# Square sums of q and k in the first mixer: the selector held in four column tiles, the squares streamed

## The reference, cut to what matters

```python
q = _causal_conv_silu(x @ w_q, conv_q)      # k likewise
q = q * rsqrt(sum(q * q, -1) + 1e-6)        # k likewise
# per token t: S = S * exp(g_t); mem = k_t S; delta = (v_t - mem) * b_t
#              S = S + k_t delta;  o_t = q_t * scale @ S
```

## Time and profile before

| what | value |
|---|---|
| median of 3 runs | 5464.05 us (5441.55 to 5478.0) |
| profiled execution, span from first to last instruction | 5452.6 us |
| time of the profiled execution beside its span | not listed apart; the median of the runs is 11.45 us above the span |
| TensorE busy with matmuls | 4831.1 us, 89% of the span |
| VectorE, ScalarE, GpSimd busy | 70%, 50%, 42% |
| mean granted TensorE clock | 0.926 |

### The profile page before, as it was taken

The page is one execution under the profiler, slowest core; times in us unless marked ns, Lnnn a source line. Parts: engine busy times, 40 slices in busy tenths (PEclk is TensorE's granted clock), DMA queues, the critical chain, the costliest instruction groups (busy, mean ns, idle before and its releaser), DMA issues. The chain is left out here.

```text
span 5452.6 us, 104905 instructions
## 1 busy us (share of the span) xinstructions
PE 4831.1 (89%) x36890; PEld 3535.1 (65%) x36890; DVE 3836.5 (70%) x9111; ACT 2736.9 (50%) x6711; POOL 2285.8 (42%) x1860
## 2 busy tenths in 40 slices
PE   5999999999999999999889989984488778998998
PEld 3787777877777787777766556641156665654665
DVE  4766667777677766767578668746699657866874
ACT  2444445444544544545478658724400116875882
POOL 2434334344334434434267347514322116743751
PEclk7999999999999999999999999986699758998998
DMA  2000000000000000000100000000000000000000
GB/s 86 5 9 7 7 9 7 7 9 7 7 9 10 5 9 8 6 9 9 34 1 0 25 5 0 0 7 0 8 1 1 1 1 30 0 24 5 0 0 16
DMA packets 170085, 52.60 MB, mean 10 GB/s; under 512 B 142304, under 2 KB 166112, under 8 KB 168928
## 3 DMA queue, kind: packets, MB, share of 16 engines
q1 hardware_dynamic: 168160, 44.30, 3.7%
q10 hardware_dynamic: 1536, 3.21, 0.2%
HBM read 36.99 MB, written 10.49 MB: 9 GB/s over the span
## 5 line engine op out<-in xcount | busy, mean ns | idle before, releaser
L799 DVE SCALAR_TENSOR_TENSOR gd_qkT<-gd_ps,gd_w_qk,gd_qkT 128x256 f32<-128x256 f32 x768 | 367.2, 482 | 193.3 <-ACT gd_qkT L632 172.7
L984 POOL TENSOR_TENSOR gd_gV<-gd_g,cst 128x512 f32<-128x512 f32 x128 | 130.3, 1040 | 860.1 <-PE gd_ps L510 860.1
L417 PE MATMUL gd_ps<-gd_taps,gd_xwins 128*128 128x512 f32 x1024 | 465.3, 597 | 0.0
L676 ACT ACTIVATE gd_X<-gd_ps 128x512 f32<-128x512 f32 x384 | 201.1, 620 | 452.9 <-PE gd_ps L496 452.6
L1540 ACT ACTIVATE L_ffn_s<-L_ffn_s,L_ffn_nb,L_ffn_r 128x128 f32<-128x128 f32 x1024 | 419.4, 482 | 3.1
L1360 POOL TENSOR_TENSOR L_ffn_t<-L_ffn_t 128x512 f32<-128x512 f32 x128 | 190.2, 1486 | 391.8 <-DVE L_ffn_t L1581 391.8
L417 PEld LDWEIGHTS gd_ps<-gd_taps,gd_xwins 128*128 128x128 f32 x1024 | 192.8, 191 | 191.1 <-issue 185.6
L868 DVE TENSOR_TENSOR gd_Z<-gd_ps,cst 128x256 f32<-128x256 f32 x384 | 162.7, 424 | 129.6 <-PE gd_ps L512 111.1
L1579 DVE TENSOR_TENSOR L_ffn_t<-L_ffn_ps,L_ffn_sb_rope 128x512 f32<-128x512 f32 x256 | 176.8, 691 | 101.8 <-PE L_ffn_ps L1385 101.8
L521 PE MATMUL gd_ps<-gd_Z,gd_X 128*128 128x64 f32 x2048 | 239.2, 275 | 0.0
L512 PE MATMUL gd_ps<-gd_gV,gd_nA 128*128 128x64 f32 x2048 | 237.9, 275 | 0.0
(11 more groups left out here) (389 smaller groups left out, 13625.6 us busy)
## 6 DMA issues: line engine op xcount, KB each, us to landing
L_ffn_sb_rope<-in_rope SPq DMA_DIRECT2D x4, 2048.0 KB, 8.3
gd_tap_row<-in_L_attn_conv_v SPq DMA_DIRECT2D x2, 2048.0 KB, 15.6
gd_blocks<-gd_nA SPq DMA_DIRECT2D x256, 16.0 KB, 1.7
gd_Z<-gd_blocks SPq DMA_DIRECT2D x32, 128.0 KB, 2.0
gd_inverses<-gd_Z SPq DMA_DIRECT2D x32, 128.0 KB, 1.7
gd_gV<-gd_inverses SPq DMA_DIRECT2D x256, 16.0 KB, 1.9
L_ffn_sb_wqkv<-in_L_ffn_wqkv SPq DMA_DIRECT2D x4, 768.0 KB, 8.9
out<-out_tok SPq DMA_DIRECT2D x8, 256.0 KB, 2.6
```

The source lines that it names most:

```text
L417: ins = pe.matmul(ps[4 + i % 2][:], xwin(j)[:, t:t + P], taps[:, t, 512 * i:512 * (i + 1)], start=(t == 0), stop=(t == TAPS - 1))
L676: act.activation(heads(X, gi).rearrange("p h x -> p (h x)"), ps[4 + gi][:], ACT.Copy).then_inc(x_s.sem, 1)
L799: ins = dve.scalar_tensor_tensor(produced(j, i), ps[6 + i % 2][:, P + t:P + t + WIDE], w_tap[:, at, t:t + 1], produced(j, i), ALU.mult, AL ...
```

## The change

The selector becomes the stationary operand: 32 columns of it, of which four carry something, in one of four column tiles (output partitions 32z to 32z + 31); the squares of a whole pair (256 tokens) stream. Pair `i` goes to tile `z = i % 4`, and the two pairs of a tile are added into the same 32 rows of bank 6, with selectors in which different columns are filled. The result is head by token, in a 128x256 area. ScalarE copies it to `sums_by_head` in SBUF, TensorE turns it back by two 128x128 transposes into columns 256 to 511 of bank 6, and VectorE reads 32 columns from there. The eight matmuls now come in one go behind `turn_k`, with the waits for the four squares; the turning comes behind the second gate projection. On ScalarE the copy stands ahead of the four `silu_gate`. The signal `square_sums_mm` counts two per chunk.

```diff
-                def square_sums(turn, q):
-                    w(sq_s.now(turn, q))
-                    for i in (2 * q, 2 * q + 1):
-                        for c in range(2):
-                            at = SUMS.start + 2 * PAIRS * c + 2 * i
-                            ins = pe.matmul(ps[6][:, at:at + 2], qk_sq[:, i, P * c:P * (c + 1)], cst[:, C_HALVES:C_HALVES + 2], start=True, stop=True)
-                    if q == 3:
-                        ins.then_inc(ss_mm.sem, 1)
+                def square_sums(turn):
+                    for i in range(PAIRS):
+                        if i % 2 == 0:
+                            w(sq_s.now(turn, i // 2))
+                        x, z = divmod(i, 4)
+                        ins = pe.matmul(ps[6][32 * z:32 * (z + 1), 0:WIDE], cst[:, C_HALVES + 32 * x:C_HALVES + 32 * (x + 1)], qk_sq[:, i], start=(x == 0), stop=(x == 1))
+                    ins.then_inc(ss_mm.sem, 1)
+
+                def turn_square_sums(turn):
+                    w(sbh_s.now(turn))
+                    for c in range(2):
+                        ins = pe.transpose(ps[6][:, SUMS.start + P * c:SUMS.start + P * (c + 1)], sums_by_head[:, P * c:P * (c + 1)], ident)
+                    ins.then_inc(ss_mm.sem, 1)
...
                 def body(n, b, c, j, s, follows, more):
                     turn_k(n, j)
-                    for i in range(4):
-                        if follows:
-                            square_sums(n + 1, i)
-                        project_gate(n, j, i)
+                    if follows:
+                        square_sums(n + 1)
+                    project_gate(n, j, 0)
+                    project_gate(n, j, 1)
+                    if follows:
+                        turn_square_sums(n + 1)
+                    project_gate(n, j, 2)
+                    project_gate(n, j, 3)
...
+                def copy_square_sums(turn):
+                    w(ss_mm.now(turn, 0))
+                    act.activation(sums_by_head[:], ps[6][:, 0:WIDE], ACT.Copy).then_inc(sbh_s.sem, 1)
...
                     token_major_k(n)
+                    if follows:
+                        copy_square_sums(n + 1)
                     for i in range(4):
                         silu_gate(n, i)
```

More of the change, by code:

```diff
@@ L29 @@
 C_HALVES = C_EYE + BASE * BASE
-C_END = C_HALVES + 2
+C_END = C_HALVES + 2 * 32
 def constant_table():
@@ L42, in constant_table @@
         t[:, C_MERGE + 64 * n:C_MERGE + 64 * (n + 1)] = i[:, None] // s == cols[None, :] // s + 1
-    t[:, C_HALVES:C_HALVES + 2] = i[:, None] // HALF == np.arange(2)[None, :]
+    for x in range(2):
+        for y in range(2):
+            t[:, C_HALVES + 32 * x + 2 * x + y] = i // HALF == y
     t[:, C_EYE:C_EYE + BASE * BASE] = np.eye(BASE).reshape(1, -1)
@@ L255, in gated_delta @@
         delta = sb("delta", [P, H, DV])
+        sums_by_head = sb("sums_by_head", [P, WIDE])
         k_ss, k_inv, k_norm, q_eps = (sb(n, [P, 2, H]) for n in ("k_ss", "k_inv", "k_norm", "q_eps"))
@@ L289, in gated_delta @@
         qk_mm, tap0_s, conv_s, silu_s = sig("qk_mm", PAIRS), sig("first_tap", PAIRS), sig("convolved", PAIRS), sig("qk_silu", PAIRS)
-        sq_s, ss_mm, ss_s, inv_k_s, nrm_s = sig("squares", 4), sig("square_sums_mm", 1), sig("square_sums", 1), sig("k_inverse", 1), sig("k_norms", 1)
+        sq_s, ss_mm, ss_s, inv_k_s, nrm_s = sig("squares", 4), sig("square_sums_mm", 2), sig("square_sums", 1), sig("k_inverse", 1), sig("k_norms", 1)
+        sbh_s = sig("sums_by_head", 1)
         v_mm, v_out, vn_s = sig("v_mm", 4), sig("v_out", 4), sig("v_scaled", 4)
@@ L313, in gated_delta @@
         PROD = slice(P, P + XWIN)
-        SUMS = slice(448, 480)
+        SUMS = slice(WIDE, 2 * WIDE)
         SCORES = slice(32, 64)
@@ L608, in _ @@
                 w(conv_s.now(0))
-                for i in range(4):
-                    square_sums(0, i)
+                square_sums(0)
+                turn_square_sums(0)
                 w(ss_s.now(0))
@@ L738, in _ @@
                 silu(0, -2, PAIRS - 1)
+                copy_square_sums(0)
                 exp_ab(1)
@@ L808, in square_sums @@
                     w(ss_mm.now(turn))
-                    sums = ps[6][:, SUMS].rearrange("p (c k two) -> p c two k", two=2, k=4)
-                    by_head = lambda t: t[:].rearrange("p c h -> p (c h)").rearrange("p (c two k) -> p c two k", two=2, k=4)
+                    sums = ps[6][:, SUMS].rearrange("p (c z g) -> p c g z", c=2, z=4)[:, :, 0:4]
+                    by_head = lambda t: t[:].rearrange("p c (g z) -> p c g z", z=4)
                     if j % 2 == 0:
```

## The result

The changed kernel takes 5389.86 us (median of 4 runs, 5378.43 to 5394.78), the kernel before 5459.01 us in the same session (4 runs, 5441.55 to 5478.0). The ratio is 0.9867, 95% interval 0.9833 to 0.9902: faster by 1.3%, 69 us. I had forecast 27 us. The span of the profiled execution fell from 5452.6 to 5385.6 us, and 66.9 of these 67.0 us are gone at the last output product of the first mixer (2702.3 us before, 2635.4 us after).

What follows compares the result with a forecast made beforehand. TensorE, busy 89% of the span, bounds the kernel, with waits deciding which savings count. Path gain -32, clock loss +20 and clock gain -15 sum to -27 us: 5464 to 5437 us (5425 to 5450; low end 5405, high end 5475).

Steps and rivals of the forecast that it cites:

- B: Every second first-mixer chunk: TensorE waits 3.05 us for the last silu, then reaches `solve` without waiting; savings up to 3.1 us count.
- 15 chunks: 32 us: In B chunks, 2.1 us less TensorE work each counts in full, 32 us saved over 15 chunks.
- The price of the four tiles: Added square matmuls, first mixer: 16 records in four column tiles take 1.1 us, with 3.5 us as the other end.
- added waits: New waits for all four squares, ScalarE's copy, its place before gate silus, and VectorE's read; priced at nothing on the path.
- A: The other chunks: TensorE waits 1.42 us at `solve` for transfers placing the inverses; saved work gains nothing, only lengthens that wait.
- I take 12 of 15, which gives back 20 us: Transfer waits in A grow to about 3.5 us, lowering the clock; about 1.7 us lost in 12 of 15, 20 us.
- term (4): VectorE reads the k sums late, holding the second half of `query_products` up to 1 us, in A alone, costing nothing.
- worth 4 to 6 us each: 15 us in all: Squares and gates behind three instruction waits: streaming squares bring the clock back sooner, 4 to 6 us each, 15 us.
- R1: Clock does not fall in A, or B's fall goes away: 47 to 60 us faster, 5404 to 5417 us; chance 0.17.
- R2: Tiles work one after another, 3.5 us for 16 records: -10 to +5 us, 5454 to 5469 us; chance 0.13.
- R4: No gain in B because transfers or ScalarE's queue are late: +5 us, 5469 us, up to 5480 us; chance 0.12.
- R3: Clock falls at A's transfer wait and stays low through `solve`'s first level: +88 us, 5552 us; chance 0.08.

Runs made afterwards that it cites:

- more in A: Changed kernel with its eight square matmuls done three times over in A chunks alone, same result: 5381.41 us, ratio 0.9865 to the kernel before.

## Why the prediction was wrong

**Right: the path in B.** "15 chunks: 32 us": an ordinary B chunk lost 2.16 us, and the 2.16 us in each of the three others, 6.5 us, with the 24.8 us of the 13 give 31 us. That nothing is lost in A or won there by the path, and that work in B counts in full, is shown by the two kernels that put work back. The price of the four tiles, taken from the row of the second mixer, was right to 0.1 us, and the rule of the Trainium skill by which a weight load overlaps a running matmul only when the row groups differ (TensorE: Matmul & The Clock Gate, "Part 3: Packing small matmuls") is not borne out by this trace: the same section's 2.38 times for three column tiles gives 1.5 us as an estimate, and 1.00 us was measured. None of the added waits showed, apart from VectorE's late read in A, which I had placed there and which costs nothing. Two readings were off without harm. I had the transfers 3.1 us ahead of TensorE in B, and in the two B chunks that now wait 1.0 us for them, they were ahead by little more than 1 us. And the six instruction waits lie at four places, so the clock fell at three of four, not at three of six.

**Wrong: "I take 12 of 15, which gives back 20 us".** This term failed. The A chunks together did not become 20 us longer, they became 4 us shorter. Three things were not as the step had it. The clock fell at the waits of A 8 and 10 times of 15, not 12, up from 3; the two waits came to 2.8 us a chunk on average, not 3.5, though to 3.1 us or more in 8 of 15. Where it fell it often cost nothing, and this is what I had missed in my own term (4): the wait comes in two pieces. A low clock that begins at the first one, of 1.1 us, slows only the products that stand ahead of the second, and the transfer wait takes that up. Three of the eight stretches of the first trace and eight of the ten of the second lay wholly ahead of the solve. And the step counted only what is new: at the silu waits, which I had left as they were, the falls went down from 12 to 6 (8 in the second trace), worth 1.6 us each. So the clock changed at two places of the loop, and I had priced one of them. A wait of 2.99 us in the A chunk above even passed without a fall; the windows in the wait and behind it:

```profile
1168.00:1172.00 4.00, 1.01 (x19) 0.82 (x16) 3.84 (x15) 1.38 (x6) 3.41 (x1) 1.00 0.20 21
1172.00:1176.00 4.00, 4.00 (x37) 4.00 (x37) 1.09 (x4) 2.06 (x4) 0.00 (x0) 1.00 0.00 0
```

Why the falls at the silu wait became fewer is not settled: the wait itself is the same 3.04 us. In the kernels with shorter transfer waits (one tile, more in A) there were 11 of them, in those with the longer ones 5 to 8, which fits an exchange between the two places, but no run was made to show what makes it.

**Too small: "worth 4 to 6 us each: 15 us in all".** The mechanism was right, the size not: 31.8 - 6.5 = 25 us in the three chunks, of which 3.6 us are the shorter instruction waits and some 22 us the clock. I had supposed that the clock would come back sooner. It did not fall there at all but for one stretch of 3.4 us in one chunk. The kernel with one tile shows the term without the shorter path.

**Left out.** Ahead of the first chunk the square sums run by themselves at a granted clock of 0.50 (from 21.9 to 80.0 us before, from 23.3 to 74.5 us after), and 3.2 us of the 5.3 us there come from them: 7.35 us from L405 to the next product, now 4.17 us. The sum had none of this. The rows, kernel before and after:

```profile
67.55 6.99 PE L405 MATMUL gd_ps<-cst,gd_delta 128*128 128x2 f32 x32 [2.12 <-DVE gd_qkT L799]
74.90 0.63 PE L411 MATMUL gd_ps<-gd_w_ab,gd_xwins 128*128 128x32 f32 x2 [0.36 <-DVE gd_k_ss L812]
```

```profile
66.02 2.63 PE L409 MATMUL gd_ps<-gd_delta,cst 128*32 128x256 f32 x16 [2.12 <-DVE gd_qkT L819]
...
70.19 0.64 PE L420 MATMUL gd_ps<-gd_w_ab,gd_xwins 128*128 128x32 f32 x2 [0.36 <-DVE gd_k_ss L832]
```

So of the 40 us between forecast and profile, 24 are the clock in A and at the silu waits, 10 the size of the term at the instruction waits, 5 the start. Each sat on the slow side, so they added up. **The rivals:** R1 (the clock does not fall in A, or B's fall goes away, 5404 to 5417 us, chance 0.17) was nearest and still 14 us too slow at its low end; the clock did fall in A, and B's falls went away in part. R2 is out by the 1.00 us, R4 by the B chunks. R3's mechanism exists, though not 15 times in a trace: once in the changed kernel's first trace and never in its second, and four times in the kernel before with the output product first. In one A chunk the clock stayed down through the first level of the solve, from L505 at 848.04 to the next L505 at 863.91 us, 15.9 us, and the granted clock was 0.54 over 18.4 us:

```profile
848.04 2.53 PE L505 MATMUL gd_ps<-cst,gd_gV 128*128 128x128 f32 x16 [2.34 <-DMA gd_gV<-gd_inverses]
850.36 6.93 PE L521 MATMUL gd_ps<-gd_gV,gd_nA 128*128 128x64 f32 x32
857.08 7.03 PE L530 MATMUL gd_ps<-gd_Z,gd_X 128*128 128x64 f32 x32
...
848.00:866.40 18.40, 18.36 (x92) 18.36 (x93) 6.04 (x22) 3.35 (x6) 0.11 (x1) 0.54 0.00 1
```

That chunk is 91.1 us long, where its neighbours of the kind are 81 to 83 us.

## What to carry to other kernels

Before pricing an edit, split the loop by which wait ends each turn: here the same 2.16 us counted in full in one chunk and not at all in the next. Try to swap a matmul with a wide stationary and a two-column stream for one that streams the wide operand, even where TensorE takes as long for it: here that kernel was 0.75% faster, for the most part by the clock. And when an edit lengthens one wait, ask whether it comes in one piece or two, and look at what the clock does at all the waits of the loop.

## What the hardware showed that I had not expected

- Being busy with matmuls does not by itself hold TensorE's clock. With the 32 two-column records in one block and TensorE busy throughout, the clock fell to 0.50 (1.2 GHz) in the block or right behind it in 22 of 30 chunks, for 3.4 or 6.8 us, without a wait for instructions near. With such records spread among the gate projections the clock, once down, stayed at 0.50 for 17 to 20 us.
- Four column tiles of 32 ran fully side by side for 32-bit floats, although the two records of each matmul go to the same tile: 16 records of 256 columns took 1.00 us and 48 took 2.72 us, so each further 16 took 0.86 us, a quarter of the 3.45 us for 16 in one tile.
- The length of a wait did not tell whether the clock falls: 2.99 us of waiting at the solve did not bring it down in one chunk, 2.34 us did in another, and there it stayed down for 17 us, with TensorE busy.
- Two queues issued transfers side by side: eight of 16 KB took 4.55 us of issue time in one queue; split, five took 2.29 us in one queue (from 1294.30) and three took 1.33 us in the other (from 1294.36).
